# Local products on eight tiles from divided probabilities, and the output projection per four batches, in a recurrent attention scan

## The chip, the cores and the metric

The kernel runs on one core of a Trainium2 chip. The metric is the device time of one execution in microseconds (us). TensorE (PE in the profile) multiplies, VectorE (DVE), ScalarE (ACT) and POOL (GpSimd) work elementwise, SyncE (SP) issues the transfers. Every engine works through its own program in order; semaphores tie them together.

## What is computed

The program computes two blocks on 16 sequences of 512 tokens of 128 features. The change touches the second block alone, `scan`. Cut to that:

```python
# xn: layernorm of x; q, k, v = split(xn @ w_qkv), 16 heads of 64
for each segment of 32 tokens, in order:
    scores = q_rope @ k_rope.T * SCALE, causal mask
    sdpa   = softmax(scores) @ v
    sq, sk = elu(q) + 1, elu(k) + 1
    out    = beta * (sq @ mem) / (sq @ z + 1e-6) + (1 - beta) * sdpa
    mem   += sk.T @ (v - (sk @ mem) / (sk @ z))
    z     += sk.sum(tokens)
x = x + concat(out) @ w_out + fp8(xn) @ fp8(weight).T + bias
```

## The kernel before

The first block and the routing take the first half of the span. `scan` walks 16 segments x 8 pairs of heads, 128 pairs `p` in all. Every instruction works on all 16 sequences at once: four sequences (`f`) lie in the four groups of 32 partitions, and four groups `g` of these along the free axis, so that 128 partitions x 512 elements hold one pair.

The work is pipelined by hand. Each engine runs a loop over steps `s`, 128 plus 5 to drain; in step `s` it does the projection of pair `s`, the scores of pair `s - 1`, the recalls and local products of pair `s - 2`, the turning of the finished heads of `s - 3`, and the output projection and memory update of `s - 4`. The order inside a step is what the code writes; an engine that waits holds up all that follows. In one step:

- TensorE: `project` of the queries (L2016), `local` (L2050: probabilities times `uu`, which holds the values, 32 matmuls of 32 x 32 weights and 64 columns), `values` (L2022), `recall` of the keys (L2032), `turn_keys` (L2068), the mask (L2056) and `score` (L2061), `project` of the keys (L2016), `recall` of the queries (L2032), `project_out` (L2080), `turn_heads` (L2073), `update` (L2040). Once per segment it turns x and its fp8 copy (L1862, L1868), multiplies for the FFN (L2155) and turns the finished output (`turn_y`, L2085). A float32 matmul is two instructions of TensorE, so `local` is 64.
- ScalarE: `features` of the queries (L2165, L2170), the copy of the turned keys (L2179) and of the values into `uu` (L2183), the exponential of the scores (L2187), `features` of the keys (L2165, L2167, L2170), the copy of the turned heads into `oT` (L2199).
- VectorE: two instructions that take the local products out of PSUM and multiply them by 1 - beta and by the reciprocal of the softmax's sum (L2247), `rope` of the queries (L2219, L2220), `sigma_q` (L2226), the key recall divided (L2257, L2259), maximum and subtraction of the scores (L2264, L2265), the query recall divided into `t2` (L2276 to L2279), `rope` of the keys, then the 32 x 32 transposes of the exponentials into `pT` (L2285), their sum (L2287) and its reciprocal (L2288), and the memory's update (L2236).
- POOL: `rotate` of the queries (L1980, L1983), `sigma_k` (L1975), the subtraction of the recalled keys from `uu` (L1995), `rotate` of the keys, and `t2` added to the local products in `ol` (L2008).

PSUM banks 0 and 1 go round among q, v, k, x, the FFN and y; 2 and 3 hold the recalls, 4 and 5 the scores, 6 the local products and both kinds of transposes, 7 the output projection, which accumulates over the eight pairs of a segment.

## Time and profile before

| | us |
|---|---|
| median of 3 runs | 3138.38 (3136.64 to 3142.13) |
| span of the profiled execution | 3131.4 |
| TensorE busy | 2658.5 (85%) |
| VectorE busy | 2510.0 (80%) |
| ScalarE busy | 1876.0 (60%) |
| POOL busy | 1754.7 (56%) |

The device time of the profiled execution is not given beside its span; the runs' median is 7.0 us above the span. The span runs from the first to the last instruction. Busy time says how long instructions lay on an engine; TensorE's matmuls overlap, and their ends are modelled. In a timeline, the difference between two starts on one engine is what a piece costs there. "Idle before" is the time in which the engine had nothing, and the arrow names what ended it.

### The profile page before, as it was taken

How to read it: one execution, taken by the hardware profiler on the slowest of the kernel's cores; microseconds unless marked ns; L12 is line 12 of the kernel's file. 1: busy time of each engine (PE TensorE's matmuls, PEld its weight loads, DVE VectorE, ACT ScalarE, POOL GpSimd, SP SyncE). 2: the span in 40 equal slices, each digit the busy share in tenths (PEclk: the TensorE clock that was granted, in tenths of full speed). 3: DMA queues.
4: the chain of work that ended last, by engine and by line, in shares of the span. 5: the costliest groups of instructions: out<-in, count | busy, mean ns of one | idle time of the engine just before them, and what ended most of it. 6: DMA issues, size and time to landing. Idle time of an engine off the chain costs nothing. (4 is left out here: it accounts for less than half of the span.)

```text
span 3131.4 us, 129400 instructions
## 1 busy us (share of the span) xinstructions
PE 2658.5 (85%) x53553; PEld 1508.1 (48%) x53553; DVE 2510.0 (80%) x7597; ACT 1876.0 (60%) x3797; POOL 1754.7 (56%) x1984
## 2 busy tenths in 40 slices
PE   5884999999999999973340899999999999999998
PEld 2441333333333333363230566666666666666665
DVE  4676899999998999766706788888888888888886
ACT  5783899999999999821000455455555555555553
POOL 5871222222222222341063788888888888888886
PEclk9895999999999999986565999999999999999999
DMA  4676344333333343094023000000000000000000
GB/s 135 235 261 178 73 106 94 93 93 99 93 90 96 94 106 94 27 276 122 0 43 89 10 12 11 8 8 11 11 11 11 11 11 11 11 11 5 11 8 11
DMA packets 179263, 209.94 MB, mean 67 GB/s; under 512 B 28592, under 2 KB 140144, under 8 KB 178416
## 3 DMA queue, kind: packets, MB, share of 16 engines
q1 hardware_dynamic: 176112, 200.25, 23.1%
q8 instruction: 427, 7.00, 1.0%
q0 software_dynamic: 2560, 1.35, 0.4%
q14 instruction: 164, 1.34, 0.1%
HBM read 125.10 MB, written 75.63 MB: 64 GB/s over the span
## 5 line engine op out<-in xcount | busy, mean ns | idle before, releaser
L829 ACT ACTIVATE at_pA<-at_ps 128x512 f32<-128x512 f32 x1024 | 551.9, 614 | 83.8 <-DVE at_ps L882 77.1
L891 DVE CUSTOM_DVE_ANT_0 at_junk<-at_ps,w_cmask 128x512 f32<-128x512 f32 (+3 forms) x1024 | 463.4, 485 | 104.4 <-PE at_ps L732 97.1
L882 DVE TENSOR_TENSOR at_ps<-at_ps,w_ratio 128x128 f32<-128x128 f32 (+3 forms) x1024 | 451.2, 491 | 4.7 <-PE at_ps L726 3.1
L701 POOL TENSOR_SCALAR_AFFINE_SELECT at_pB<-at_pB 128x128 f32<-128x128 f32 x256 | 75.4, 294 | 639.6 <-ACT at_pB L835 637.5
L835 ACT ACTIVATE at_pB<-at_ps 128x512 f32<-128x512 f32 (+1 forms) x768 | 379.4, 531 | 53.0 <-PE at_ps L739 47.7
L1980 POOL TENSOR_TENSOR sc_rb<-sc_rb,v_sin 128x512 f32<-128x512 f32 x256 | 326.6, 1276 | 37.6 <-DVE sc_ra L2220 36.2
L2016 PE MATMUL sc_ps<-sc_xT,v_wqkv 128*128 128x512 f32 x512 | 286.1, 641 | 3.9 <-PEq L56 1.4
L726 PE MATMUL at_ps<-at_aq,at_ak 72*128 72x512 bf16 x1024 | 278.3, 388 | 2.7 <-DMA at_ak<-parts_scratch 2.4
L2179 ACT COPY sc_skN<-sc_ps 128x512 f32<-128x512 f32 x128 | 75.1, 587 | 323.6 <-PE sc_ps L2068 323.6
L1975 POOL TENSOR_TENSOR sc_sk<-sc_ee,sc_relu 128x512 f32<-128x512 f32 x128 | 167.0, 1304 | 180.5 <-ACT sc_ee L2170 180.3
L739 PE MATMUL at_ps<-at_bq,at_bk 75*128 75x512 bf16 (+3 forms) x1024 | 265.7, 302 | 1.5 <-ACT at_pB L835 0.9
L759 PE MATMUL at_ps<-at_pA,at_v 128*32 128x512 f32 x2048 | 263.0, 609 | 1.2 <-ACT at_oT L818 1.2
L732 PE MATMUL at_ps<-at_bk,at_bq 72*128 72x512 bf16 (+3 forms) x1024 | 225.1, 306 | 43.8 <-DMA at_bk<-parts_scratch 35.2
L2165 ACT ACTIVATE sc_ee<-sc_ps 128x512 f32<-128x512 f32 x256 | 150.4, 587 | 110.2 <-PE sc_ps L2016 109.0
L2219 DVE STREAM_SHUFFLE sc_rb<-sc_ps 128x512 f32<-128x512 f32 x256 | 189.1, 739 | 0.0
L2050 PEld LDWEIGHTS sc_ps<-v_uu,sc_pT 32*32 32x32 f32 x8192 | 125.4, 105 | 116.2 <-issue 109.1
L2220 DVE TENSOR_TENSOR sc_ra<-sc_ps,v_cos 128x512 f32<-128x512 f32 x256 | 172.3, 673 | 0.0
L1983 POOL TENSOR_TENSOR sc_kr<-sc_ra,sc_rb 128x512 f32<-128x512 f32 x128 | 163.1, 1274 | 10.0
L1983 POOL TENSOR_TENSOR sc_qr<-sc_ra,sc_rb 128x512 f32<-128x512 f32 x128 | 162.7, 1271 | 10.0
L2236 DVE TENSOR_TENSOR v_mem<-v_mem,sc_ps 128x520 f32<-128x520 f32 x256 | 161.8, 674 | 6.6 <-PE sc_ps L2040 6.6
L2008 POOL TENSOR_TENSOR sc_ol<-sc_ol,sc_t 128x512 f32<-128x512 f32 x128 | 163.2, 1275 | 5.9 <-DVE sc_t L2279 5.9
L2170 ACT ACTIVATE sc_ee<-sc_ee 128x512 f32<-128x512 f32 x256 | 161.4, 631 | 8.2
(316 smaller groups left out, 5937.4 us busy)
## 6 DMA issues: line engine op xcount, KB each, us to landing
parts_scratch<-fr_parts SPq DMA_DIRECT2D x64, 384.0 KB, 4.1
at_bq<-parts_scratch SPq DMA_DIRECT2D x192, 96.0 KB
at_bk<-parts_scratch SPq DMA_DIRECT2D x192, 96.0 KB
at_aq<-parts_scratch SPq DMA_DIRECT2D x192, 96.0 KB
at_ak<-parts_scratch SPq DMA_DIRECT2D x192, 96.0 KB
v_scratch<-fr_v SPq DMA_DIRECT2D x32, 352.0 KB, 4.3
at_v<-v_scratch SPq DMA_DIRECT2D x32, 352.0 KB, 3.6
parts_scratch<-fr_parts SPq DMA_DIRECT2D x32, 256.0 KB, 3.9
```

The lines of the kernel that those rows point to most:

```text
L726: pe.matmul(ps[:, BANK[f"A{j}"], :], ak[:, slot, n % 4, j * P:(j + 1) * P], aq[:, slot, n % 4], start=True, stop=True).then_inc(filled, 1)
L732: ins = pe.matmul(ps[:, BANK[kind], col:col + wide], bq[0:ROWS, slot, n % 4, j * P:(j + 1) * P], bk[0:ROWS, slot, n % 4, 0:wide], start=Tr ...
L739: ins = pe.matmul(ps[:, BANK[kind], col:col + S - j * P], bk[:, slot, n % 4, j * P:(j + 1) * P], bq[:, slot, n % 4, j * P:S], start=True, ...
L759: ins = pe.matmul(ps[32 * s:32 * s + 32, PV, q0:S], v[:, b % 2, a, j, h * (HD + 1):h * (HD + 1) + 32], probs, start=(j == 0), stop=(j == N ...
L829: act.activation(pA[:, n % A_RING, j * S:(j + 1) * S], src, ACT.Exp).then_inc(exped, 1)
L835: act.activation(pB[:, n % T_RING, at:at + wide], src[:, 0:wide], ACT.Exp).then_inc(exped, 1)
L882: dve.tensor_tensor(src[:, 0:wide], src[:, 0:wide], W["ratio"][:, S - wide:S], ALU.mult).then_inc(tilted, 1)
L891: ins = dve.tensor_tensor_reduce(junk[:, P * j * (j + 1) // 2:P * (j + 1) * (j + 2) // 2], src[:, col:col + wide], W["cmask"][:, S - wide: ...
L1980: pool.tensor_tensor(by_pos(rb[:, n % 2]), by_pos(rb[:, n % 2]), table("sin", which), ALU.mult).then_inc(G["sn"], 1)
L1983: pool.tensor_tensor(rot[which][:, p % 2], ra[:, n % 2], rb[:, n % 2], ALU.add).then_inc(G["add_d"], 1)
L2016: pe.matmul(ps[:, bank_of("qk"[which], p), :], V["wqkv"][:, col:col + P], xT[:, p // PAIRS % 2], start=True, stop=True).then_inc(G["pj"], 1)
L2219: dve.stream_shuffle(rb[:, n % 2], x, [lane ^ 1 for lane in range(32)])
```

## The change

1. `local` writes two banks instead of one. For the even groups `g` the products of the partitions of `f` go to the output partitions of `f`, in bank 6, as before; for the odd groups they go to those of `f ^ 1`, in bank 7. So there are eight pairs of rows and columns of the array in use instead of four. The query recall, the FFN's input (`take_xq`, three copies instead of one), the residual `hb` and the stored `y` follow that order of the partitions.
2. The probabilities are divided before they are multiplied. VectorE takes the sum and reciprocal before `rope` of the keys, POOL multiplies (a new instruction of 128 x 256), and VectorE transposes after `rope`.
3. ScalarE, no longer VectorE, takes the local products out of PSUM, scaled by 1 - beta; VectorE, no longer POOL, adds `t2`.
4. The output projection holds the tokens as weights. `oT` keeps all eight pairs of two segments. In each step from the 11th on, one half of one group `g` (four pairs) of a segment that is complete is multiplied: 4 matmuls of 128 columns into a quarter of bank 7. VectorE adds each half to `y` (128 x 128), and `local` and `project_out` of the next step wait for that (`ydone`). `turn_y`, the copy `yT` and the addition of 128 x 512 go.
5. The residual is loaded by transfers of its own into `hb` (`load_hb`), and stores are eight transfers per segment instead of four. The drain takes 10 steps instead of 5.

```diff
-        oT, yT = sb("oT", [P, 2, S]), sb("yT", [P, S])
+        oT = sb("oT", [P, 2, PAIRS, S])
...
+        by_ch = lambda ap: ap.rearrange("p (h g) -> p g h", h=2)
+        swapped = lambda g, f: f ^ (g % 2)
+        YCOL = 256
...
+        def load_hb(sp, seg, j):
+            for f in range(B1):
+                for odd in range(2):
+                    to = 32 * swapped(odd, f)
+                    sp.dma_start(hb[to:to + 32, j % 2, odd::2], h_seg[f, bass.ds(seg, 1)].rearrange("o i g d -> (o i) g d")[:, odd::2]).then_inc(G[f"hb_in{j % 2}"], 16)
...
-            wait_h(pool, j)
-            pool.tensor_tensor(hb[:, j % 2], ht[:, j % 2], V["bias"][:].unsqueeze(1).broadcast_to([P, BG, D]), ALU.add).then_inc(G["hb_d"], 1)
+            wait(pool, f"hb_in{j % 2}", 128 * max(1, (j + 1) // 2))
+            pool.tensor_tensor(hb[:, j % 2], hb[:, j % 2], V["bias"][:].unsqueeze(1).broadcast_to([P, BG, D]), ALU.add).then_inc(G["hb_d"], 1)
...
-            act.copy(xqT[:, j % 2], ps[:, bank, 0:256].bitcast(BF16)).then_inc(G["xqt_c"], 1)
+            place = lambda ap: ap.rearrange("p (q o a b i) -> p q o a b i", q=2, o=2, a=2, b=2)
+            to, at = place(xqT[:, j % 2]), place(ps[:, bank, 0:256].bitcast(BF16))
+            act.copy(to[:, :, 0].rearrange("p q a b i -> p q (a b i)"), at[:, :, 0].rearrange("p q a b i -> p q (a b i)"))
+            for b in range(2):
+                ins = act.copy(to[:, :, 1, :, 1 - b], at[:, :, 1, :, b])
+            ins.then_inc(G["xqt_c"], 1)
...
-        STEPS = PT + 5
+        HALVES, AFTER = 2 * BG, PAIRS + 2
+        STEPS = PT + AFTER
...
+        out_half = lambda s: (divmod((s - AFTER) % HALVES, 2), (s - AFTER) // HALVES) if inside(s - AFTER) else None
...
                     for j in range(PER):
-                        wait(sp, "ydone", j + 1)
-                        for f in range(B1):
-                            sp.dma_start(o_seg[f, bass.ds(seg + j, 1)].rearrange("o i g d -> (o i) g d"), y[32 * f:32 * f + 32, j % 2]).then_inc(G[f"stored{j % 2}"], 16)
                         if j + 3 in readied:
                             wait(sp, "xnn_d", j + 1)
-                            wait(sp, "hb_d", j + 1)
                             load(sp, seg + j + 3, j + 3)
+                        if j + 2 in readied:
+                            wait(sp, "ffn_c", j + 1)
+                            load_hb(sp, seg + j + 2, j + 2)
+                        wait(sp, "ydone", HALVES * (j + 1))
+                        for f in range(B1):
+                            for odd in range(2):
+                                at = 32 * swapped(odd, f)
+                                sp.dma_start(o_seg[f, bass.ds(seg + j, 1)].rearrange("o i g d -> (o i) g d")[:, odd::2], y[at:at + 32, j % 2, odd::2]).then_inc(G[f"stored{j % 2}"], 16)
...
+                            wait(pool, "smd", p + 1)
+                            probs = ss[:, p % 2].rearrange("p (g h) j -> p g h j", h=2)
+                            pool.tensor_tensor(probs, probs, bc(by_ch(sm[:, p % 4]), SEG), ALU.mult).then_inc(G["nrm"], 1)
...
-                            wait(pool, "ffn_c", j - 1)
                             add_bias(pool, j)
-                        p = s - 2
-                        if inside(p):
-                            wait(pool, "qd", p + 1)
-                            wait(pool, "old", p + 1)
-                            o = ol[:, p % 4].rearrange("p g h d -> p (g h d)")
-                            pool.tensor_tensor(o, o, t2[:, p % 2].rearrange("p c d -> p (c d)"), ALU.add).then_inc(G["od"], 1)
 
...
-                                    ins = pe.matmul(ps[32 * f:32 * f + 32, 2 + hh, g * VE:(g + 1) * VE],
+                                    to = 32 * (swapped(g, f) if which == 0 else f)
+                                    ins = pe.matmul(ps[to:to + 32, 2 + hh, g * VE:(g + 1) * VE],
...
                     def local(p):
-                        for g in range(BG):
-                            for hh in range(2):
+                        for hh in range(2):
+                            for g in range(BG):
                                 for f in range(B1):
-                                    ch = 2 * g + hh
-                                    ins = pe.matmul(ps[32 * f:32 * f + 32, 6, ch * DH:(ch + 1) * DH], pT[32 * f:32 * f + 32, p % 4, ch, :],
+                                    ch, to, col = 2 * g + hh, 32 * swapped(g, f), (2 * (g // 2) + hh) * DH
+                                    ins = pe.matmul(ps[to:to + 32, 6 + g % 2, col:col + DH], pT[32 * f:32 * f + 32, p % 4, ch, :],
                                                     uu[32 * f:32 * f + 32, p % PAIRS, g, hh, 0:DH], start=True, stop=True)
...
-                    def project_out(p):
-                        wait(pe, "otc", p + 1)
-                        wait(pe, "yt_c", p // PAIRS)
-                        h = p % PAIRS
-                        pe.matmul(ps[:, 7, :], V["wout"][:, h], oT[:, p % 2], start=(h == 0), stop=(h == PAIRS - 1)).then_inc(G["oproj"], 1)
-
-                    def turn_y(bank, j):
-                        wait(pe, "yt_c", j + 1)
-                        for g in range(BG):
-                            ins = pe.transpose(ps[:, bank, g * P:(g + 1) * P], yT[:, g * P:(g + 1) * P], V["ident"][:])
-                        ins.then_inc(G["yt"], 1)
+                    def project_out(j, g, half):
+                        few = range(half * PAIRS // 2, (half + 1) * PAIRS // 2)
+                        for h in few:
+                            ins = pe.matmul(ps[:, 7, YCOL:YCOL + D], oT[:, j % 2, h, g * P:(g + 1) * P], V["wout"][:, h], start=(h == few[0]), stop=(h == few[-1]))
+                        ins.then_inc(G["oproj"], 1)
...
+                            wait(pe, "ydone", s - AFTER)
                             wait(pe, "pt", p + 1)
                             local(p)
...
-                        p = s - 4
-                        if inside(p):
-                            project_out(p)
+                        if out_half(s):
+                            (g, half), j = out_half(s)
+                            wait(pe, "old", min(s - 1, PT))
+                            wait(pe, "otc", j * PAIRS + 4 * half + 4)
+                            wait(pe, "ydone", s - AFTER)
+                            project_out(j, g, half)
...
+                            wait(act, "pvd", p + 1)
+                            wait(act, "ott", p - 3)
+                            local = ps[:, 6:8, 0:256].rearrange("p b (q h d) -> p b q h d", h=2, d=DH)
+                            to = ol[:, p % 4].rearrange("p (q b) h d -> p b q h d", b=2)
+                            for hh in range(2):
+                                col = 2 * (p % PAIRS) + hh
+                                ins = act.activation(to[:, :, :, hh], local[:, :, :, hh], ACT.Identity, scale=V["rest"][:, col:col + 1])
+                            ins.then_inc(G["old"], 1)
...
-                            wait(dve, "pvd", p + 1)
-                            wait(dve, "pt", p + 1)
-                            wait(dve, "ott", p - 3)
-                            local = ps[:, 6, :].rearrange("p (g h d) -> p g h d", h=2, d=DH)
-                            for hh in range(2):
-                                col = 2 * (p % PAIRS) + hh
-                                ins = dve.scalar_tensor_tensor(ol[:, p % 4, :, hh], local[:, :, hh], V["rest"][:, col:col + 1],
-                                                               bc(head(sm[:, p % 4])[:, hh], DH), ALU.mult, ALU.mult)
-                            ins.then_inc(G["old"], 1)
...
+                        p = s - 3
+                        if inside(p):
+                            wait(dve, "old", p + 1)
+                            wait(dve, "qd", p + 1)
+                            o = ol[:, p % 4].rearrange("p g h d -> p (g h d)")
+                            dve.tensor_tensor(o, o, t2[:, p % 2].rearrange("p c d -> p (c d)"), ALU.add).then_inc(G["od"], 1)
...
+                        p = s - 1
+                        if inside(p):
+                            wait(dve, "se", p + 1)
+                            s_ = sm[:, p % 4]
+                            link(dve.tensor_reduce(head(s_), by_head(ss[:, p % 2]), AX.X, ALU.add))
+                            dve.reciprocal(s_, s_).then_inc(G["smd"], 1)
                         if s < PT:
                             rope(2 * s + 1)
                         p = s - 1
                         if inside(p):
-                            wait(dve, "se", p + 1)
-                            dve.transpose(pT[:, p % 4].rearrange("p c j -> p (c j)"), ss[:, p % 2].rearrange("p c j -> p (c j)"))
-                            s_ = sm[:, p % 4]
-                            link(dve.tensor_reduce(head(s_), by_head(ss[:, p % 2]), AX.X, ALU.add))
-                            dve.reciprocal(s_, s_).then_inc(G["pt"], 1)
+                            wait(dve, "nrm", p + 1)
+                            dve.transpose(pT[:, p % 4].rearrange("p c j -> p (c j)"), ss[:, p % 2].rearrange("p c j -> p (c j)")).then_inc(G["pt"], 1)
                         if s - 7 in starts:
                             j = (s - 7) // PAIRS
                             wait(dve, "ffn", j + 1)
                             wait(dve, "hb_d", j)
-                            wait(dve, f"stored{j % 2}", 64 * (j // 2))
+                            wait(dve, f"stored{j % 2}", 128 * (j // 2))
                             dve.scalar_tensor_tensor(flat(y[:, j % 2]), ps[:, bank_of("ffn", j), :], V["qs"][:, 4:5], flat(hb[:, j % 2]),
                                                      ALU.mult, ALU.add).then_inc(G["ffn_c"], 1)
-                        if s - 12 in starts:
-                            j = (s - 12) // PAIRS
-                            wait(dve, "yt", j + 1)
+                        if out_half(s):
+                            (g, half), j = out_half(s)
+                            wait(dve, "oproj", s - AFTER + 1)
                             wait(dve, "ffn_c", j + 1)
-                            dve.tensor_tensor(flat(y[:, j % 2]), flat(y[:, j % 2]), ps[:, bank_of("y", j), :], ALU.add).then_inc(G["ydone"], 1)
+                            wait(dve, "ydone", s - AFTER)
+                            dve.tensor_tensor(y[:, j % 2, g], y[:, j % 2, g], ps[:, 7, YCOL:YCOL + D], ALU.add).then_inc(G["ydone"], 1)
```

The order on POOL in the steady state, from the rotation of the queries to that of the next step's. `sc_sk` is what `sigma_k` writes, `v_uu` the subtraction's, `sc_ss` the probabilities, `sc_ol` the local products. Before:

```order
L1980 TENSOR_TENSOR sc_rb<-sc_rb,v_sin 128x512
L1983 TENSOR_TENSOR sc_qr<-sc_ra,sc_rb 128x512
L1975 TENSOR_TENSOR sc_sk<-sc_ee,sc_relu 128x512
L1995 TENSOR_TENSOR v_uu<-v_uu,sc_t 128x8x64
L1980 TENSOR_TENSOR sc_rb<-sc_rb,v_sin 128x512
L1983 TENSOR_TENSOR sc_kr<-sc_ra,sc_rb 128x512
L2008 TENSOR_TENSOR sc_ol<-sc_ol,sc_t 128x512
```

With the change:

```order
L2001 TENSOR_TENSOR sc_rb<-sc_rb,v_sin 128x512
L2004 TENSOR_TENSOR sc_qr<-sc_ra,sc_rb 128x512
L1996 TENSOR_TENSOR sc_sk<-sc_ee,sc_relu 128x512
L2016 TENSOR_TENSOR v_uu<-v_uu,sc_t 128x8x64
L2021 TENSOR_TENSOR sc_ss<-sc_ss,sc_sm 128x256
L2001 TENSOR_TENSOR sc_rb<-sc_rb,v_sin 128x512
L2004 TENSOR_TENSOR sc_kr<-sc_ra,sc_rb 128x512
```

The addition into `sc_ol` is gone from the end, and the multiply of the probabilities stands behind the subtraction from `v_uu`.

The order on VectorE from the maximum of the scores to the memory's update (`sc_mx` maximum, `sc_rq` reciprocal of the query recall, `sc_sm` sums, `sc_pT` the transposed probabilities). Before:

```order
L2264 TENSOR_REDUCE sc_mx<-sc_ps 128x8
L2265 TENSOR_TENSOR sc_ss<-sc_ps,sc_mx 128x2x4x32
L2276 SCALAR_TENSOR_TENSOR sc_rq<-sc_ps,v_ibeta 128x8
L2277 RECIPROCAL sc_rq<-sc_rq 128x8
L2279 TENSOR_TENSOR sc_t<-sc_ps,sc_rq 128x2x4x64
L2219 STREAM_SHUFFLE sc_rb<-sc_ps 128x512
L2220 TENSOR_TENSOR sc_ra<-sc_ps,v_cos 128x512
L2285 STREAM_TRANSPOSE sc_pT<-sc_ss 128x256
L2287 TENSOR_REDUCE sc_sm<-sc_ss 128x8
L2288 RECIPROCAL sc_sm<-sc_sm 128x8
L2236 TENSOR_TENSOR v_mem<-v_mem,sc_ps 128x2x4x65 x2
```

With the change:

```order
L2273 TENSOR_REDUCE sc_mx<-sc_ps 128x8
L2274 TENSOR_TENSOR sc_ss<-sc_ps,sc_mx 128x2x4x32
L2286 TENSOR_TENSOR sc_ol<-sc_ol,sc_t 128x512
L2291 SCALAR_TENSOR_TENSOR sc_rq<-sc_ps,v_ibeta 128x8
L2292 RECIPROCAL sc_rq<-sc_rq 128x8
L2294 TENSOR_TENSOR sc_t<-sc_ps,sc_rq 128x2x4x64
L2299 TENSOR_REDUCE sc_sm<-sc_ss 128x8
L2300 RECIPROCAL sc_sm<-sc_sm 128x8
L2239 STREAM_SHUFFLE sc_rb<-sc_ps 128x512
L2240 TENSOR_TENSOR sc_ra<-sc_ps,v_cos 128x512
L2306 STREAM_TRANSPOSE sc_pT<-sc_ss 128x256
L2319 TENSOR_TENSOR sc_y<-sc_y,sc_ps 128x128
```

Sum and reciprocal stand before the rotation, the transpose behind it, and the addition of a finished half to `sc_y` follows the transpose.

## Rows read from the trace of the kernel before

**Rows 1.** The page, busy us (share of span) and slices of the span: TensorE

```profile
PE 2658.5 (85%) x53553; PEld 1508.1 (48%) x53553; DVE 2510.0 (80%) x7597; ACT 1876.0 (60%) x3797; POOL 1754.7 (56%) x1984
...
PEclk9895999999999999986565999999999999999999
```

**Rows 2.** The view of line L2050 (`local`), all of it

```profile
L2050 PE MATMUL sc_ps<-v_uu,sc_pT x8192: 211/214/312, 1739.9 to 3114.3; 32*32 32x64 f32 x200
```

**Rows 3.** Timeline of one step, TensorE: start us, us busy, engine, line, instructions [idle before]

```profile
2043.46 1.10 PE L2050 MATMUL sc_ps<-v_uu,sc_pT 32*32 32x64 f32 x64
...
2044.50 1.16 PE L2022 MATMUL sc_ps<-v_wqkv,sc_xT 128*128 128x128 f32 x8
...
2045.58 0.86 PE L2032 MATMUL sc_ps<-v_mem,sc_sk 64*32 64x65 f32 x64
...
2046.38 0.66 PE L2068 MATMUL sc_ps<-v_ident,sc_sk 128*128 128x128 f32 x4
...
2047.07 0.71 PE L2061 MATMUL sc_ps<-sc_kr,sc_qr 64*32 64x32 f32 x59
...
2048.58 0.25 PE L2061 MATMUL sc_ps<-sc_kr,sc_qr 64*32 64x32 f32 x5 [0.80 <-issue]
2048.76 1.12 PE L2016 MATMUL sc_ps<-sc_xT,v_wqkv 128*128 128x512 f32 x2
...
2050.61 1.13 PE L2080 MATMUL sc_ps<-sc_oT,v_wout 128*128 128x512 f32 x2
...
2054.19 0.60 PE L2050 MATMUL sc_ps<-v_uu,sc_pT 32*32 32x64 f32 x28
```

**Rows 4.** Timeline of the same step, the other engines

```profile
2051.16 0.69 DVE L2279 TENSOR_TENSOR sc_t<-sc_ps,sc_rq 128x512 f32<-128x512 f32 x1
2051.22 0.63 ACT L2170 ACTIVATE sc_ee<-sc_ee 128x512 f32<-128x512 f32 x1
...
2051.93 1.28 POOL L1975 TENSOR_TENSOR sc_sk<-sc_ee,sc_relu 128x512 f32<-128x512 f32 x1 [2.49 <-ACT sc_ee L2170]
...
2053.00 0.43 DVE L2285 STREAM_TRANSPOSE sc_pT<-sc_ss 128x256 f32<-128x256 f32 x1
2053.16 1.19 POOL L1995 TENSOR_TENSOR v_uu<-v_uu,sc_t 128x512 f32<-128x512 f32 x1
...
2053.36 0.37 DVE L2287 TENSOR_REDUCE sc_sm<-sc_ss 128x8 f32<-128x256 f32 x1
```

**Rows 5.** Timeline of another step: T and `sigma_k`

```profile
2416.86 1.12 PE L2016 MATMUL sc_ps<-sc_xT,v_wqkv 128*128 128x512 f32 x2
...
2420.38 1.28 POOL L1975 TENSOR_TENSOR sc_sk<-sc_ee,sc_relu 128x512 f32<-128x512 f32 x1 [1.70 <-ACT sc_ee L2170]
```

**Rows 6.** Groups by form: line engine op out<-in xcount | busy, mean ns | idle before

```profile
L1980 POOL TENSOR_TENSOR sc_rb<-sc_rb,v_sin 128x512 f32<-128x512 f32 x256 | 326.6, 1276 | 37.6 <-DVE sc_ra L2220 36.2
...
L704 POOL TENSOR_SCALAR_AFFINE_SELECT at_pB<-at_pB 128x384 f32<-128x384 f32 x256 | 133.8, 523 | 0.1
...
L241 POOL TENSOR_TENSOR fr_sc<-fr_sc 128x8 f32<-128x8 f32 x8 | 1.6, 203 | 0.0
...
L864 DVE TENSOR_TENSOR at_on<-at_ps,at_rr 128x128 f32<-128x128 f32 x128 | 37.4, 292 | 4.4
...
L835 ACT ACTIVATE at_pB<-at_ps 128x256 f32<-128x256 f32 x256 | 98.1, 383 | 0.0
```

**Rows 7.** Groups by form of the window 1735 to 3115 us, TensorE

```profile
L2050 PE MATMUL sc_ps<-v_uu,sc_pT 32*32 32x64 f32 x8192 | 147.0, 216 | 15.9 <-DVE sc_sm L2288 9.7 <-issue 3.5
...
L2032 PE MATMUL sc_ps<-v_mem,sc_sk 64*32 64x65 f32 x8184 | 116.0, 225 | 14.0 <-issue 13.8
...
L2061 PE MATMUL sc_ps<-sc_kr,sc_qr 64*32 64x32 f32 x8154 | 103.3, 199 | 15.7 <-issue 15.0
```

**Rows 8.** Timeline of the end, ScalarE and VectorE

```profile
3122.36 0.59 ACT L2199 COPY sc_oT<-sc_ps 128x512 f32<-128x512 f32 x1 [1.75 <-PE sc_ps L2073]
...
3127.08 0.68 DVE L2300 TENSOR_TENSOR sc_y<-sc_y,sc_ps 128x512 f32<-128x512 f32 x1
```

28 lines of the change are left out of this document (11 added, 17 removed).

## The prediction, as made before the run

> **What bounds the kernel now.** I began with the page's busy shares and its slices [rows 1]. TensorE is busiest with 85% of the span, and from the 23rd slice (22 x 78.3 = 1722 us) to the last its clock stands at nine tenths or more of full speed, so at the 2.4 GHz level nearly throughout. The change touches only `scan`, which begins there, so I looked at nothing else. Next the rows of the line of `local`, which runs once per step (a step is one pair of heads of one segment; there are 128): the 128 bursts begin between 1739.9 and 3114.3 us, and the last burst begins at about 3113.4, so one step takes (3113.4 - 1739.9) / 127 = **10.82 us** [rows 2].
>
> Then I took one ordinary step apart. On TensorE [rows 3] it runs from the first `local` at 2043.46 to the next at 2054.19, which is 10.73 us. Start to start: `local` 1.04, values 1.08, recall of the keys 0.80, `turn_keys` and mask 0.69, `score`, and only then the projection of the keys, whose start I call T (2048.76). `score` took 1.69, of which 1.00 was a stop in its middle with no wait in the program (the profile says "issue"): its first 59 instructions take 0.51 without the last one's own 0.20, the other five 0.18, so 0.69 packed. Local to T is thus 4.30 packed and 5.30 here. From T: key projection and recall of the queries 1.85, output projection 0.96, then `turn_heads`, update, the transposes of one ready segment and the next query projection, up to T + 5.43, where the next `local` starts. So TensorE is nearly packed; I read it as the bound, with VectorE (80% of the whole span) close behind.
>
> On the other engines [rows 4] the same step has a chain which starts at T. ScalarE gets the projected keys and does two Relus and an Exp, the Exp starting at T + 2.46; POOL can then start `sigma_k` at T + 3.17 and, right behind it, the subtraction from `uu`, which ends at T + 5.59 (2053.16 + 1.19). Before the change nobody who holds up `local` waits for that: `local` needs the transposed probabilities, which VectorE begins at T + 4.24. This is where the change bites.
>
> **The change, part by part.**
>
> *Division of the probabilities on POOL.* The sum and the reciprocal move ahead of the rotation on VectorE, then POOL multiplies, then VectorE transposes. POOL runs strictly in program order, and the new multiply stands behind `sigma_k` and the subtraction from `uu`. So its inputs may be ready at about T + 3.7 (t2 ends at T + 3.1 [rows 4], then a sum and a reciprocal), but it starts at the end of the subtraction: T + 5.59 in this step. In another step `sigma_k` started at T + 3.52 instead of T + 3.17 [rows 4, 5], which with the same 2.42 for the two makes T + 5.94; VectorE was late there with work that the change takes off it, so I take 5.67. Nothing in the trace shows the multiply. Its nearest rows on POOL are 523 ns for a select over 384 elements per lane and 1276 ns for a multiply of 512 with a broadcast operand; an 8-element multiply takes 203 ns [rows 6]. The line between 203 and 1276 gives 203 + 1073 x 248/504 = 731 ns for its 256 elements. I take **0.73**, between 0.52 and 1.28.
>
> *What then stands before `local`.* A handoff to VectorE (0.08, as from the Exp's end at 2051.85 to `sigma_k` at 2051.93 [rows 4]), the transpose (0.36 start to start [rows 4]), and, new, the addition of the finished half of the output, since `local` also waits for `ydone` of the step before: 292 ns for 128 x 128 [rows 6], and 0.10 for the handoff to TensorE. Sum 0.73 + 0.08 + 0.36 + 0.29 + 0.10 = 1.56. In one step of eight the FFN's instruction on 512 elements stands between the transpose and that addition; at the 0.68 of a like-sized addition [rows 8] that is 0.09 on average. `local` then starts at T + 5.67 + 1.56 + 0.09 = **T + 7.32**, where the packed TensorE would be there at T + 5.4. Nothing covers that wait: all of TensorE is queued behind it, values, recalls and the next T included, and ScalarE, POOL and VectorE wait for these. The wait closes a loop: T, ScalarE, POOL, VectorE, `local`, next T.
>
> *Eight tiles instead of four in `local`.* Before, 64 instructions start every 16 ns on four tiles (1.04 us). The recalls, also 64 instructions, of 65 columns on eight tiles and two banks, take 0.80; `score` with 32 columns takes 0.69 [rows 3]. I take 0.80: **-0.24** inside the loop. Bounds: -0.35 and 0. The profile shows four tiles in different row groups writing one bank with starts 16 ns apart and 214 ns each [rows 2, 3], so they do overlap. The Trainium skill (TensorEngine Tiling (Array Packing), Restrictions and Gotchas) says that different row tiles cannot access the same bank at the same time. The new form still has four row groups in each of two banks. By that rule `local` would not get shorter. It is the third rival.
>
> *The loop's length.* Local to T: 4.30 - 0.24 = 4.06, plus pauses. TensorE idles 14.0 us before the key recall and 15.7 us before `score` in 128 steps, 0.23 per step; the listing sees 0.80 of the 1.00 lost in the example [rows 3, 7], so 0.30. The step becomes 4.06 + 0.30 + 7.32 = **11.68 us**, 0.86 more than 10.82. Over 125 steps: **+107 us**. The pauses in the other half (recall of the queries) vanish in the wait and are not in this sum.
>
> *Output projection, tokens held.* Four matmuls of 128 columns (two instructions each, like the values' 1.08) for one of 512 (0.96 [rows 3]): +0.12 per step, between T and `local`, where there are now 1.9 us of slack: nothing. The four transposes of `turn_y` and the copy of `yT` per segment go, also there: nothing. Hidden by the wait for the probabilities; without it the sum would be -0.24 + 0.12 - 0.06 = -0.18 per step.
>
> *Evacuation of the local products.* From two VectorE instructions (0.80 us) to two ScalarE ones. A 128 x 256 activation from PSUM takes 383 ns [rows 6]. They start when `local` ends and `turn_keys` needs them 1.9 us after that (values and key recall); 0.8 us fits. The addition into `ol` moves from POOL to VectorE, in the gap in which VectorE waits for the query recall. POOL and VectorE both get less work than before. Nothing.
>
> *More DMAs.* The residual is loaded a second time (8 transfers per segment), the stores are 8 instead of 4. They are issued some steps ahead; DMA is nearly idle in `scan`. Nothing, but for half a microsecond behind the last store.
>
> *The end.* The last 8 halves of the projection come out one per step with nothing beside them: after the last copy into `oT` seven remain, each 1.08 of matmuls, 0.2 until the result is there, 0.29 addition, 0.1 handoff, 1.65 x 7 = 11.6. Before, from that copy's end (3122.36 + 0.59) to the end of the last addition (3127.08 + 0.68) it took 4.8 [rows 8]. With the longer chain in the two draining steps and half a microsecond of stores I take **+10**.
>
> Sum: 107 + 10 = +117. The span shown is 3131.4; the median of the runs is 3138.4, 7 us more, which I keep. Forecast 3138.4 + 117 = **3255 us**.
>
> **The rivals.**
> 1. *The multiply is covered and TensorE stays the bound.* Then only TensorE's sum counts: -0.18 x 128 = -23, and +10 at the end: 3125, faster. The point from which it decides: POOL's path must deliver `local` no later than TensorE itself gets there, mean 10.82 - 4.60 = T + 6.2 with the pauses; it needs 1.1 us less than my 7.32. For it: the wait ends only 1.1 us after the mean. Against: POOL's subtraction alone ends at T + 5.6 in an undisturbed step, before multiply, transpose and addition. 9%.
> 2. *The pauses before T disappear*, since TensorE's queue fills while it waits: 0.30 x 125 = 38 less: 3217. For it: they come in dense stretches. 20%.
> 3. *Eight tiles are no faster than four*: 0.24 x 128 = +31: 3286. 10%.
> 4. *The multiply costs as much as one of 512*: +0.55 x 125 = +69: 3324. 8%.
> 5. *It balances out*, rival 1 with half its gain lost to new waits in one step of eight (the rounding of a segment delays VectorE, and the addition into `ol` with it): about 3138. 3%.
>
> **How the numbers follow.** My forecast has 50%, with the rivals 9, 20, 10, 8 and 3. Cheapest plausible combination of bounds: multiply 0.52 (-26), no pauses (-38): 3191, so the range begins at 3190; it ends at 3325 with rival 4. A measurement of this kernel can tell about 0.2%, some 6 us, from no change. Faster 0.09, same 0.03, slower 0.88.
>
> **What would show it.** TensorE's idle time in front of `local` should rise from 15.9 us [rows 7] to over 150, released by VectorE (its transpose or the half's addition), and POOL's new multiply should start within 0.1 us of the end of the subtraction. `local` should take 0.8 us; the idle time before the query recall should stay or shrink. POOL and VectorE shares of `scan` fall while the step grows to 11.7 us. I am wrong if the step is under 10.8 us, or if the multiply is not found right behind the subtraction, or if `local` is found waiting for ScalarE.

## The result, and the profile after

The changed kernel takes **3269.7 us** (median of 4 runs, 3265.8 to 3282.8) where the kernel before takes 3140.3 in the same comparison (4 runs, 3136.6 to 3144.0): a ratio of 1.0416, 95% interval 1.0394 to 1.0439. Its profiled execution has a span of 3263.6 us against 3131.4. One run of the kernel before, among those beside e5 to e8, took 3725.1 us at a mean granted clock of 0.64 (0.93 in the others) and is left out of all ratios. The page's busy shares and granted clock:

```profile
PE 2660.1 (82%) x54257; PEld 1561.6 (48%) x54257; DVE 2513.9 (77%) x7581; ACT 1973.7 (60%) x4069; POOL 1674.9 (51%) x1984
...
PEclk9995999999999999865658999999999999999999
```

TensorE lies as long in its instructions as before (2660.1 us against 2658.5) in a span that is 132 us longer, and its granted clock in the loop is nearly the same (0.99 from 1800 to 3100 us, 1.00 before): the time is waiting. The line of `local`, with what ended TensorE's idle time before it (us, times):

```profile
L2070 PE MATMUL sc_ps<-v_uu,sc_pT x8192: 210/215/312, 1743.3 to 3234.7; 32*32 32x64 f32 x200
...
  DVE sc_y L2319: 112.2, 100
  DVE sc_pT L2306: 22.7, 9
```

Before, the idle time there was 15.9 us in all [rows 7]. The groups of the whole scan stretch (busy us and mean ns, then idle us before them and who ended it), of TensorE and then of the new chain:

```profile
L2052 PE MATMUL sc_ps<-v_mem,sc_sq 64*32 64x65 f32 x8192 | 120.6, 225 | 24.7 <-issue 23.1 <-DVE sc_t L2268 1.0
...
L2052 PE MATMUL sc_ps<-v_mem,sc_sk 64*32 64x65 f32 x8192 | 118.0, 228 | 23.6 <-issue 23.6
L2070 PE MATMUL sc_ps<-v_uu,sc_pT 32*32 32x64 f32 x8192 | 115.1, 226 | 127.9 <-DVE sc_y L2319 112.2 <-DVE sc_pT L2306 13.7 <-issue 1.9
...
L2021 POOL TENSOR_TENSOR sc_ss<-sc_ss,sc_sm 128x256 f32<-128x256 f32 x128 | 80.5, 629 | 3.6 <-DVE sc_sm L2300 3.6
...
L2306 DVE STREAM_TRANSPOSE sc_pT<-sc_ss 128x256 f32<-128x256 f32 x128 | 57.0, 445 | 105.5 <-POOL sc_ss L2021 104.5
```

Idle before `local` is 127.9 us, ended by VectorE's addition of the half (L2319) or its transpose (L2306). The transpose itself waits 105.5 us, for POOL's multiply; the multiply waits 3.6, so POOL's program holds it, not its inputs. An ordinary step, from one `local` to the next (start, duration):

```profile
2131.74 0.85 PE L2070 MATMUL sc_ps<-v_uu,sc_pT 32*32 32x64 f32 x64 [0.34 <-DVE sc_y L2319]
...
2133.60 0.69 PE L2052 MATMUL sc_ps<-v_mem,sc_sk 64*32 64x65 f32 x45
...
2135.01 0.41 PE L2052 MATMUL sc_ps<-v_mem,sc_sk 64*32 64x65 f32 x19 [0.71 <-issue]
...
2136.74 1.12 PE L2035 MATMUL sc_ps<-sc_xT,v_wqkv 128*128 128x512 f32 x2
...
2137.80 0.57 PE L2052 MATMUL sc_ps<-v_mem,sc_sq 64*32 64x65 f32 x35
...
2139.06 0.45 PE L2052 MATMUL sc_ps<-v_mem,sc_sq 64*32 64x65 f32 x29 [0.69 <-issue]
...
2139.90 1.28 POOL L1996 TENSOR_TENSOR sc_sk<-sc_ee,sc_relu 128x512 f32<-128x512 f32 x1 [3.12 <-ACT sc_ee L2184]
...
2141.14 1.19 POOL L2016 TENSOR_TENSOR v_uu<-v_uu,sc_t 128x512 f32<-128x512 f32 x1
...
2142.28 0.63 POOL L2021 TENSOR_TENSOR sc_ss<-sc_ss,sc_sm 128x256 f32<-128x256 f32 x1
...
2142.94 0.45 DVE L2306 STREAM_TRANSPOSE sc_pT<-sc_ss 128x256 f32<-128x256 f32 x1 [0.40 <-POOL sc_ss L2021]
...
2143.31 0.25 DVE L2319 TENSOR_TENSOR sc_y<-sc_y,sc_ps 128x128 f32<-128x128 f32 x1
...
2143.66 0.38 PE L2070 MATMUL sc_ps<-v_uu,sc_pT 32*32 32x64 f32 x19 [0.72 <-DVE sc_y L2319]
```

T is 2136.74. `sigma_k` (L1996) starts at T + 3.16, the subtraction (L2016) ends at T + 5.59, and the multiply stands in POOL's queue right behind it, at T + 5.54 (the records of POOL overlap by 0.05). It takes 0.63; transpose, addition and handoffs take 0.75 more, and `local` starts at T + 6.92, after a wait of 0.72. In this step both recalls (L2052) have a stop without a wait, of 0.7 us.

The end of the span, with the halves of the output projection one after the other, and TensorE's granted clock in it (the column before the DMA share):

```profile
3242.70 1.97 PE L2099 MATMUL sc_ps<-v_wout,sc_oT 128*128 128x128 f32 x8
...
3245.53 0.59 ACT L2219 COPY sc_oT<-sc_ps 128x512 f32<-128x512 f32 x1 [3.36 <-PE sc_ps L2093]
...
3255.32 1.13 PE L2099 MATMUL sc_ps<-v_wout,sc_oT 128*128 128x128 f32 x8 [0.47 <-DVE sc_y L2319]
...
3256.92 1.13 PE L2099 MATMUL sc_ps<-v_wout,sc_oT 128*128 128x128 f32 x8 [0.47 <-DVE sc_y L2319]
3258.09 0.29 DVE L2319 TENSOR_TENSOR sc_y<-sc_y,sc_ps 128x128 f32<-128x128 f32 x1 [1.31 <-PE sc_ps L2099]
```

```profile
3240.00:3245.00 5.00, 4.81 (x82) 4.20 (x80) 2.47 (x5) 0.58 (x1) 0.00 (x0) 0.56 0.19 46
3245.00:3263.60 18.60, 10.06 (x188) 8.60 (x187) 4.43 (x11) 0.59 (x1) 0.00 (x0) 0.94 0.07 17
```

**Where the 132 us of span lie.** The first `local` starts 3.4 us later (1739.9, then 1743.3). The first instruction of the last `local` moves from 3113.4 to 3232.0, so that 127 steps take 1488.7 us instead of 1373.5: 11.72 each instead of 10.82, **115.2 us**. From there to the end it is 31.6 us instead of 18.0: **13.6**. The first term is hardly the change's: over all kernels below, the first `local` starts between 1737.5 and 1750.0, and for the nine that have this change's transfers and output projection between 1737.5 and 1745.8. What moves it is not isolated; the clock in the 23 us before it is low in both kernels, 0.80 here (the third column from the end) and 0.82 before:

```profile
1722.00:1745.00 23.00, 12.57 (x167) 7.84 (x168) 12.27 (x35) 10.09 (x21) 12.86 (x11) 0.80 0.13 36
```

### The profile page after: what moved, and what is told of

Read it like the earlier page. It is cut to its first block and busy times, and to the rows that moved or that the text cites. A ratio compares the mean times of both kernels' runs of the same rounds, so it can differ in the third digit from the quotient of the medians.

```text
span 3263.6 us, 131202 instructions
## 1 busy us (share of the span) xinstructions
PE 2660.1 (82%) x54257; PEld 1561.6 (48%) x54257; DVE 2513.9 (77%) x7581; ACT 1973.7 (60%) x4069; POOL 1674.9 (51%) x1984
## 3 DMA queue, kind: packets, MB, share of 16 engines
q14 instruction: 169, 1.38, 0.2%
## 5 line engine op out<-in xcount | busy, mean ns | idle before, releaser
L1996 POOL TENSOR_TENSOR sc_sk<-sc_ee,sc_relu 128x512 f32<-128x512 f32 x128 | 170.5, 1332 | 330.5 <-ACT sc_ee L2184 330.5
L2035 PE MATMUL sc_ps<-sc_xT,v_wqkv 128*128 128x512 f32 x512 | 291.8, 653 | 17.0 <-DVE sc_ra L2240 12.8
L2070 PE MATMUL sc_ps<-v_uu,sc_pT 32*32 32x64 f32 x8192 | 115.1, 226 | 127.9 <-DVE sc_y L2319 112.2
L2070 PEld LDWEIGHTS sc_ps<-v_uu,sc_pT 32*32 32x32 f32 x8192 | 94.3, 105 | 231.6 <-issue 220.8
L2240 DVE TENSOR_TENSOR sc_ra<-sc_ps,v_cos 128x512 f32<-128x512 f32 x256 | 172.6, 674 | 0.0
```

Of the source, the lines that this page charges most:

```text
L1996: pool.tensor_tensor(sig[1][:, p % 4], ee[:, 1], relu[:], ALU.add).then_inc(G["sgk"], 1)
L2035: pe.matmul(ps[:, bank_of("qk"[which], p), :], V["wqkv"][:, col:col + P], xT[:, p // PAIRS % 2], start=True, stop=True).then_inc(G["pj"], 1)
```

## The experiments

All ratios are to the kernel before, run beside them on the same chip. "Step" is the mean over 110 steps, from the starts of `local`; A is the part from `local` to T, B from T to the next `local`; "stops" is the time per step in pauses inside TensorE's bursts that no wait explains; then TensorE's busy time per step, and its idle time per step that the profile says VectorE ended, before whatever instruction. These are worked out from all TensorE records of a trace. The last three do not add up to the step exactly: ends of matmuls are modelled, and short gaps are left out.

| kernel | us | ratio, 95% interval | step | A | B | stops | TensorE busy | waits for VectorE | last `local` to end |
|---|---|---|---|---|---|---|---|---|---|
| before | | 1 | 10.83 | 4.77 | 6.05 | 0.71 | 10.04 | 0.18 | 18.0 |
| changed | 3269.7 | 1.0416 (1.0394 to 1.0439) | 11.71 | 4.59 | 7.12 | 0.66 | 9.95 | 1.19 | 31.6 |
| e1 | 3203.3 | 1.0216 (1.0189 to 1.0242) | 11.26 | 4.76 | 6.50 | 0.97 | 9.93 | 0.48 | 31.6 |
| e2 | 3243.5 | 1.0354 (1.0332 to 1.0376) | 11.58 | 4.63 | 6.95 | 0.83 | 9.90 | 0.97 | 31.4 |
| e3 | 3275.7 | 1.0452 (1.0430 to 1.0474) | 11.83 | 4.71 | 7.12 | 0.61 | 10.12 | 1.17 | 31.5 |
| e4 | 3187.3 | 1.0171 (1.0144 to 1.0199) | 11.15 | 4.73 | 6.42 | 0.93 | 9.94 | 0.38 | 31.4 |
| e5 | 3150.7 | 1.0084 (1.0068 to 1.0101) | 10.85 | 4.50 | 6.35 | 0.65 | 9.91 | 0.39 | 31.5 |
| e6 | 3151.3 | 1.0083 (1.0061 to 1.0105) | 10.89 | 4.59 | 6.30 | 0.50 | 10.07 | 0.41 | 31.4 |
| e7 | 3257.4 | 1.0423 (1.0397 to 1.0449) | 11.73 | 4.66 | 7.07 | 0.41 | 10.18 | 1.21 | 17.5 |
| e8 | 3363.9 | 1.0771 (1.0743 to 1.0800) | 12.53 | 4.85 | 7.67 | 0.36 | 10.37 | 1.84 | 31.2 |
| e9 | 3144.3 | 1.0034 (1.0019 to 1.0048) | 10.87 | 4.65 | 6.22 | 0.51 | 10.04 | 0.37 | 17.1 |
| e10 | 3131.8 | 1.0001 (0.9986 to 1.0016) | 10.76 | 4.51 | 6.25 | 0.36 | 10.06 | 0.39 | 18.4 |
| e11 | 3151.0 | 1.0050 (1.0029 to 1.0071) | 10.88 | 4.44 | 6.45 | 0.64 | 9.44 | 0.94 | 28.0 |

The kernel before takes 3132.7 beside e1 to e4 (7 runs), 3124.0 beside e5 to e8 (11), 3132.3 beside e9 to e11 (26). So times of different groups are compared by their ratios.

### e1: the multiply ahead of the subtraction from `uu`

```diff
                             sigma_k(s)
+                        p = s - 1
+                        if inside(p):
+                            wait(pool, "smd", p + 1)
...
+                            pool.tensor_tensor(probs, probs, bc(by_ch(sm[:, p % 4]), SEG), ALU.mult).then_inc(G["nrm"], 1)
                         p = s - 2
...
                             pool.tensor_tensor(new, new, t1[:, p % 2].rearrange("p (g h) d -> p g h d", h=2), ALU.subtract).then_inc(G["ud"], 1)
-                        p = s - 1
-                        if inside(p):
-                            wait(pool, "smd", p + 1)
...
```

> The changed kernel (3269.7 us) with one thing moved: POOL multiplies the probabilities behind sigma_k and before the subtraction from uu, not behind it. Theory (loop T, ScalarE, POOL, VectorE, local): the multiply starts at about T + 4.4 (or when the reciprocal is ready, T + 3.8 to 4.6) instead of T + 5.6, the addition of the half ends 0.7 us later or a bit more, and local is reached at about T + 6.2, mostly TensorE's own time. The step falls from 11.7 to about 10.7 us, 127 steps, so 3145 us, range 3115 to 3165. Rival (the cost lies in TensorE's own work, the output projection in 128-column pieces or the new tile order): within 10 us of 3270.

About half of the loss goes (1.0416 to 1.0216), not nearly all of it. A step of e1, the T of which is 2130.15:

```profile
2130.15 1.13 PE L2035 MATMUL sc_ps<-sc_xT,v_wqkv 128*128 128x512 f32 x2
...
2132.10 0.17 DVE L2291 SCALAR_TENSOR_TENSOR sc_rq<-sc_ps,v_ibeta 128x8 f32<-128x8 f32 x1 [0.36 <-PE sc_ps L2052]
...
2132.90 1.05 PE L2099 MATMUL sc_ps<-v_wout,sc_oT 128*128 128x128 f32 x8 [0.84 <-issue]
...
2134.35 0.68 DVE L2240 TENSOR_TENSOR sc_ra<-sc_ps,v_cos 128x512 f32<-128x512 f32 x1
...
2134.54 0.63 POOL L2015 TENSOR_TENSOR sc_ss<-sc_ss,sc_sm 128x256 f32<-128x256 f32 x1
...
2135.16 1.13 PE L2035 MATMUL sc_ps<-sc_xT,v_wqkv 128*128 128x512 f32 x2
2135.20 0.45 DVE L2306 STREAM_TRANSPOSE sc_pT<-sc_ss 128x256 f32<-128x256 f32 x1 [0.17 <-POOL sc_ss L2015]
2135.57 0.25 DVE L2319 TENSOR_TENSOR sc_y<-sc_y,sc_ps 128x128 f32<-128x128 f32 x1
...
2136.22 0.98 PE L2070 MATMUL sc_ps<-v_uu,sc_pT 32*32 32x64 f32 x64
```

The multiply now starts at T + 4.39, but `local` only at T + 6.07. In this step it does not wait at all: it follows the projection of the queries (2135.16), and TensorE had stopped for 0.84 us ahead of `project_out`. Over the scan a wait is left, less than a third of the changed kernel's:

```profile
L2070 PE MATMUL sc_ps<-v_uu,sc_pT 32*32 32x64 f32 x8192 | 116.0, 223 | 39.9 <-DVE sc_y L2319 24.4 <-DVE sc_pT L2306 8.8 <-issue 6.2
```

VectorE works down a program of its own that starts when the query recall lands: its division, `t2`, the sum (L2299), the reciprocal, the rotation (L2240 ends it), and only then the transpose and the addition (L2306, L2319). In the step shown it ends 0.4 us before TensorE gets to `local`; in others it ends later. The mean of B falls by 0.62 only. By the table e1's step is 0.43 longer than the kernel before's for two reasons of like size: 0.30 more waits for VectorE, and 0.26 more stops, with 0.11 less busy time against them.

### e2: the half's addition ahead of the transpose

```diff
                             rope(2 * s + 1)
+                        if out_half(s):
...
+                            dve.tensor_tensor(y[:, j % 2, g], y[:, j % 2, g], ps[:, 7, YCOL:YCOL + D], ALU.add).then_inc(G["ydone"], 1)
                         p = s - 1
                         if inside(p):
                             wait(dve, "nrm", p + 1)
...
-                        if out_half(s):
...
```

> The changed kernel with VectorE's addition of the finished half moved ahead of its wait for the multiplied probabilities, so that the addition lies in that wait. Theory: the 0.25 us start to start (and the FFN's instruction's share, no longer between transpose and addition) leave the loop: 0.3 us in some 118 steps, -35 us, so 3235 us; local is then released by the transpose. Rival (local waits for the products of something else, or the end of the addition is not what it waits for): 3270.

The addition's input (from L2099) has long been there, so it fits in front of the wait for POOL: 0.6% come back, 20 us of the 35 expected. B falls by 0.17, and the stops grow by as much (0.66 to 0.83), partly in A. `local` now waits for the transpose alone:

```profile
L2070 PE MATMUL sc_ps<-v_uu,sc_pT 32*32 32x64 f32 x8192 | 113.6, 223 | 105.7 <-DVE sc_pT L2312 103.8 <-issue 1.6
```

### e3: four tiles in `local` again

```diff
-        swapped = lambda g, f: f ^ (g % 2)
+        swapped = lambda g, f: f
...
-                ins = act.copy(to[:, :, 1, :, 1 - b], at[:, :, 1, :, b])
+                ins = act.copy(to[:, :, 1, :, b], at[:, :, 1, :, b])
```

> The changed kernel with local on the four diagonal tiles again, still alternating between the two banks, all partitions in their old order. Theory: local takes 1.04 instead of 0.80 us, inside the loop, so +0.24 x 127 = +30 us, 3300 us. Rival (TensorE is not on the loop in this part, or two banks and not eight tiles shorten local): 3270.

The burst takes 1.03 us instead of 0.78 (medians to the next instruction), inside the loop, where the wait stays as long:

```profile
L2070 PE MATMUL sc_ps<-v_uu,sc_pT 32*32 32x64 f32 x8192 | 147.4, 218 | 125.6 <-DVE sc_y L2319 110.5 <-DVE sc_pT L2306 13.7 <-issue 1.3
```

Since e3 keeps the two banks, it is the eight tiles and not the second bank that shorten the burst. Of the 0.25 only 0.12 reach the step: 0.4% of the time by the runs (its interval just overlaps the changed kernel's), 15 us by the traces, instead of the 31 that 0.24 x 128 gives. In e5 against e6 they bring nothing.

### e4: the division left out

```diff
-                            pool.tensor_tensor(probs, probs, bc(by_ch(sm[:, p % 4]), SEG), ALU.mult).then_inc(G["nrm"], 1)
...
-                            wait(dve, "nrm", p + 1)
+                            wait(dve, "smd", p + 1)
```

Its output lacks the division of the softmax; the sum and reciprocal are still worked out.

> The changed kernel without POOL's multiply: the probabilities stay undivided (that part of the computation is left out), VectorE transposes when its rotation is done. Theory: local is reached at about T + 5.8 to 6.2, where TensorE's own work with its pauses ends; step 10.5 to 10.6 us, so about 3130 us, and nearly the same as with the early multiply. Rival (TensorE's own work carries the loss): above 3240.

Even without the multiply 1.7% stay, where the theory expected nothing. Of the 1.7%, 0.4 are the drain. The wait before `local` is 28.1 us, against 15.9 in the kernel before:

```profile
L2065 PE MATMUL sc_ps<-v_uu,sc_pT 32*32 32x64 f32 x8192 | 115.7, 223 | 28.1 <-DVE sc_y L2314 14.4 <-DVE sc_pT L2301 7.7 <-issue 4.9
```

By the table the step is 0.32 longer than before: 0.20 more waits for VectorE (before `local`, `turn_heads` and a projection) and 0.22 more stops, with 0.10 less busy time. That VectorE's new *order* costs without the new instruction is therefore not shown: e5, with another order, waits for VectorE as long (0.39), and what it has less than e4 is stops (0.65 against 0.93).

### e5 and e6: all of it off the chain

VectorE takes sum and reciprocal while it waits for the query recall; POOL multiplies while it waits for ScalarE's exponential, ahead of `sigma_k`; VectorE transposes and adds the half ahead of the rotation. e6 is the same with e3's four tiles.

```diff
                             rotate(2 * s)
+                        p = s - 1
+                        if inside(p):
+                            wait(pool, "smd", p + 1)
...
+                            pool.tensor_tensor(probs, probs, bc(by_ch(sm[:, p % 4]), SEG), ALU.mult).then_inc(G["nrm"], 1)
                         if s < PT:
                             sigma_k(s)
...
+                            link(dve.tensor_reduce(head(s_), by_head(ss[:, p % 2]), AX.X, ALU.add))
+                            dve.reciprocal(s_, s_).then_inc(G["smd"], 1)
                         p = s - 2
                         if inside(p):
                             wait(dve, "qr_s", p + 1)
...
+                            wait(dve, "nrm", p + 1)
...
+                            dve.tensor_tensor(y[:, j % 2, g], y[:, j % 2, g], ps[:, 7, YCOL:YCOL + D], ALU.add).then_inc(G["ydone"], 1)
                         if s < PT:
                             rope(2 * s + 1)
```

> The changed kernel with VectorE's sum and reciprocal moved into its wait for the query recall, POOL's multiply ahead of sigma_k (POOL is idle there), and VectorE's transpose and the half's addition ahead of its rotation of the keys. No instruction is added or left out. Theory: local can start from about T + 4 on, so that the loop is gone and TensorE's own work is the bound: 9.55 us packed plus the stops inside bursts, which were 0.7 per step before and 0.97 in e1, so a step of 10.5 and about 3120 us, range 3095 to 3150; idle before local under 20 us in all. Rival (the loss sits in the new output projection and its additions): still above 3180.

> As e5, with local on four tiles. Theory: with TensorE as the bound the 0.24 us of local count in every step, less what the stops give back: e3 cost 0.12 per step with the loop, of which 0.24 is local and -0.1 are fewer stops. Between +10 and +30 us over e5. Rival (eight tiles bring nothing, since a denser burst only meets a later block of instructions): within 5 us of e5.

With the same instructions in this order 3.3% come back, and 0.8% stay. In e5's scan the wait before `local` is gone, and the transpose no longer waits for POOL:

```profile
L2060 PE MATMUL sc_ps<-v_uu,sc_skN 32*64 32x65 f32 x8192 | 122.0, 234 | 30.9 <-DVE sc_t L2300 26.2 <-issue 3.7 <-DVE v_mem L2256 0.5
...
L2070 PE MATMUL sc_ps<-v_uu,sc_pT 32*32 32x64 f32 x8192 | 114.7, 224 | 9.2 <-issue 5.2 <-DVE sc_pT L2304 3.3
...
L2093 PE MATMUL sc_ps<-v_ident,sc_ol 128*128 128x128 f32 x512 | 79.1, 277 | 17.2 <-DVE sc_ol L2286 15.4 <-issue 1.8
...
L2304 DVE STREAM_TRANSPOSE sc_pT<-sc_ss 128x256 f32<-128x256 f32 x128 | 55.7, 435 | 2.5 <-POOL sc_ss L2013 2.5
```

The loop is back at 10.85 against 10.83. The span differs from before by 21.4: 2.8 in the loop, 5.1 before the first `local`, 13.5 after the last. The theory expected 3120. Its idle time before `local` came out, but TensorE still waits 0.39 us per step for VectorE in other places (before the update and `turn_heads` above all), which the theory left out. The multiply isn't quite free for POOL either: on average it ends at T + 3.47, and `sigma_k` starts at T + 3.61 instead of T + 3.18, but the loop does not show it (10.85).

e6 is equal to e5: its rival came true. TensorE is busy 0.16 us longer per step and stops 0.15 less.

### e7: the kernel before, with the division alone

Sum and reciprocal before the rotation, POOL's multiply behind the subtraction, the transpose after the rotation; tiles, projection and evacuation of the kernel before (its evacuation without the reciprocal).

```diff
+                            wait(pool, "smd", p + 1)
+                            probs = ss[:, p % 2].rearrange("p (g h) j -> p g h j", h=2)
+                            pool.tensor_tensor(probs, probs, bc(sm[:, p % 4].rearrange("p (h g) -> p g h", h=2), SEG), ALU.mult).then_inc(G["nrm"], 1)
...
-                                ins = dve.scalar_tensor_tensor(ol[:, p % 4, :, hh], local[:, :, hh], V["rest"][:, col:col + 1],
-                                                               bc(head(sm[:, p % 4])[:, hh], DH), ALU.mult, ALU.mult)
+                                ins = dve.tensor_scalar(ol[:, p % 4, :, hh], local[:, :, hh], V["rest"][:, col:col + 1], None, ALU.mult)
```

> The kernel before with one part of the change alone: sum and reciprocal before VectorE's rotation, POOL's multiply behind the subtraction from uu, the transpose after the rotation, the local products then scaled by 1 - beta alone. Output projection, tiles and the engines of evacuation stay as they were. Theory: local at T + 5.6 + 0.63 + 0.05 + 0.45 + 0.1 = T + 6.8, the step 4.7 + 6.8 = 11.5 to 11.6 us, so +90 us on the kernel before: 3225, range 3200 to 3250. Rival (the loss needs the new output projection): within 20 us of the kernel before.

This one part gives the **whole** loss, 1.0423, with the same step (11.73) and the same wait:

```profile
L2055 PE MATMUL sc_ps<-v_uu,sc_pT 32*32 32x64 f32 x8192 | 151.6, 222 | 127.0 <-DVE sc_pT L2295 126.5
...
L2000 POOL TENSOR_TENSOR sc_ss<-sc_ss,sc_sm 128x256 f32<-128x256 f32 x128 | 80.5, 629 | 4.0 <-DVE sc_sm L2289 4.0
```

It is more than the 90 us expected: the multiply starts at T + 5.72 on average where the theory had 5.6, and `local` at T + 7.07 where it had 6.8. In the loop the rest takes as much as it gives: the eight tiles give 0.12 per step (e3), the half's addition in the chain takes 0.13 (e2). Only the drain is left, 17.5 us here against 31.6: the span of e7 is 3253.1, 10.5 less than the changed kernel's, which the ratios, from different groups, don't resolve.

### e8: the multiply twice

```diff
+                            pool.tensor_tensor(waste[:].rearrange("p (g h) j -> p g h j", h=2), probs, bc(by_ch(sm[:, p % 4]), SEG), ALU.mult)
                             pool.tensor_tensor(probs, probs, bc(by_ch(sm[:, p % 4]), SEG), ALU.mult).then_inc(G["nrm"], 1)
```

> The changed kernel with POOL's multiply done twice (once into a buffer that nobody reads). Theory: POOL's multiply lies on the loop at full price, +0.59 us start to start in 127 steps, +75 us on the changed kernel: 3340. Rival (the multiply is partly covered): clearly less, under +45.

The step grows by 0.82, more than the 0.59 between the starts of the two multiplies. The group of `local` in e8, and its window of the scan:

```profile
L2072 PE MATMUL sc_ps<-v_uu,sc_pT 32*32 32x64 f32 x8192 | 118.0, 232 | 209.1 <-DVE sc_y L2321 187.4 <-DVE sc_pT L2308 20.5 <-issue 1.2
```

```profile
1800.00:3330.00 1530.00, 1262.55 (x42909) 932.16 (x42908) 1136.96 (x2783) 769.59 (x1525) 1097.47 (x1004) 0.94 0.04 11
```

The wait before `local` grows by 81 us, 0.64 per step, which is the multiply; it lies in B, which grows by 0.55. A grows by 0.26. The rest is TensorE itself: its granted clock over the scan is 0.94, where the changed kernel has 0.99. It idles longer in each step, and in part of the steps it is then at the 1.2 GHz level: values and projections last longer (1.38 instead of 1.12 us per step for the values).

### e9: the kernel before, with only sum and reciprocal early

```diff
+                            wait(dve, "se", p + 1)
+                            s_ = sm[:, p % 4]
+                            link(dve.tensor_reduce(head(s_), by_head(ss[:, p % 2]), AX.X, ALU.add))
+                            link(dve.reciprocal(s_, s_))
                         p = s - 2
                         if inside(p):
                             wait(dve, "qr_s", p + 1)
...
-                            link(dve.tensor_reduce(head(s_), by_head(ss[:, p % 2]), AX.X, ALU.add))
-                            dve.reciprocal(s_, s_).then_inc(G["pt"], 1)
```

> The kernel before, with one thing moved: VectorE adds the two halves of the sums of exponentials and takes their reciprocals before it waits for the recalled query, as in e5. The transposition follows, then the rope's addition; nothing else changes. Theory (in the kernel before, VectorE's chain that starts when the query's recall lands is late at the local product by 15.9 us over the loop, 0.12 us per step, and the two small operations on it are worth about 0.2): the idle time before the local product falls below 8 us and the kernel takes 3118 to 3132 us where the kernel before takes 3132, a ratio of 0.996 to 1.000. Rival (the same chain also feeds VectorE's next work, which TensorE waits for elsewhere): ratio under 0.994. Rival (the reciprocal now waits for ScalarE's exponential and holds the query's addition up): over 1.002.

```profile
L2050 PE MATMUL sc_ps<-v_uu,sc_pT 32*32 32x64 f32 x8192 | 145.4, 217 | 8.1 <-DVE sc_pT L2290 6.4 <-issue 1.6
...
L2040 PE MATMUL sc_ps<-v_uu,sc_skN 32*64 32x65 f32 x8192 | 119.8, 232 | 49.0 <-DVE sc_t L2285 45.6 <-issue 1.7 <-DVE v_mem L2236 0.5
```

The same line of the kernel before, in the same stretch:

```profile
L2040 PE MATMUL sc_ps<-v_uu,sc_skN 32*64 32x65 f32 x8192 | 120.6, 232 | 24.1 <-DVE sc_t L2279 19.5 <-issue 4.0 <-DVE v_mem L2236 0.5
```

The wait before `local` halves [rows 7], and the one before the memory's update (L2040), which needs the query recall done with (L2285), goes from 24.1 to 49.0: the sum and the reciprocal now stand ahead of that division. It is 0.3% slower, as the last rival had it, and the theory of a gain falls. Of that the loop accounts for 7 us (1380.3 against 1373.5); its first `local` also starts 10 us later in the trace. VectorE's chain feeds TensorE in two places, and moving work from one to the other is no gain.

### e10: the division off the chain, projection and tiles of before

e6 with `project_out`, `turn_y`, `yT`, residual and stores of the kernel before:

```diff
-                            project_out(j, g, half)
+                            project_out(p)
...
-                            act.copy(oT[:, p // PAIRS % 2, p % PAIRS], ps[:, 6, :]).then_inc(G["otc"], 1)
+                            act.copy(oT[:, p % 2], ps[:, 6, :]).then_inc(G["otc"], 1)
```

> e6 (four tiles; sum, reciprocal, multiply, transposition and addition off the chain, as in e5) with the output projection of the kernel before: no tokens held, one projection per two batches and its old evacuation. So it is the kernel before with the division made on the probabilities, off the chain. Theory (the last 0.8% of e5 and e6 over the kernel before are the held tokens' longer drain, 31.5 us against 18.0, and some 0.1 us per step of the projection per four batches): the drain is back at 18 to 20 us, the step is 10.75 to 10.85, and the time is 3125 to 3140 us where the kernel before takes 3132, ratio 0.998 to 1.002. Rival (the division itself costs outside the chain, by the VectorE and GpSimd work it adds to the step): the loop stays at 10.89 and only the drain comes back: ratio 1.003 to 1.006. Rival (the chain off the query's recall was the bound of the kernel before too): ratio under 0.996.

```profile
L2049 PE MATMUL sc_ps<-v_uu,sc_pT 32*32 32x64 f32 x8192 | 142.9, 216 | 4.2 <-DVE sc_pT L2292 3.3 <-issue 0.9
```

1.0001, interval 0.9986 to 1.0016: no difference from the kernel before. The drain is 18.4 us, and the step 10.76, 0.13 less than e6. So the 0.8% of e6 is the new output projection with its residual and stores: its drain (13 us) and 0.1 us per step. The latter isn't matmul work: TensorE is busy as long in both (10.06 and 10.07); the stops are 0.36 instead of 0.50. And the division, placed so and with ScalarE's evacuation, costs nothing on balance: against the kernel before TensorE waits 0.21 us more per step for VectorE and stops 0.35 less. Nothing tried beats the kernel before by more than the measurement can tell.

### e11: e5 with a quarter of the output projection

One of the four matmuls of each half is left; the output lacks the other three pairs' parts.

```diff
-                        for h in few:
-                            ins = pe.matmul(ps[:, 7, YCOL:YCOL + D], oT[:, j % 2, h, g * P:(g + 1) * P], V["wout"][:, h], start=(h == few[0]), stop=(h == few[-1]))
+                        for h in (few[0],):
+                            ins = pe.matmul(ps[:, 7, YCOL:YCOL + D], oT[:, j % 2, h, g * P:(g + 1) * P], V["wout"][:, h], start=True, stop=True)
```

> e5 with three of the four matmuls of each half of the output projection left out, so that its output lacks those parts of the sum. TensorE's output projection (2.33 us per step) falls to about 0.6. Theory (with the division off the chain TensorE's own work is the bound again, nothing else is near it): nearly all of it comes back, 1.6 us per step over 120 steps, and 2 us in the drain: 2950 to 2990 us where e5 has 3151. Rival (the step is held by the chain through softmax, query recall and transposition, just under TensorE's work): less than half of it comes back, the idle time before the local product is back above 60 us, and the time is over 3060. Rival (stops inside TensorE's bursts shrink with the instructions they depend on): under 2940.

The expectation's 2.33 us per step for the projection was wrong: it is 151.6 us in all in e5, 1.2 per step, and 65.5 here. But even these 86 us bring nothing in the loop: its step is 10.88, not less. Part of them TensorE does not gain at all: its granted clock from 1800 to 3100 us is 0.97 where e5 has 0.99, its other groups take longer (L2060: 241 ns instead of 234), and its busy time falls by 0.47 us per step, 60 us in the loop. The 0.3% to e5 are its drain (28.0 us) and a first `local` 4.3 us earlier.

```profile
L2060 PE MATMUL sc_ps<-v_uu,sc_skN 32*64 32x65 f32 x8192 | 126.0, 241 | 73.8 <-DVE sc_t L2300 68.4 <-issue 4.2 <-DVE v_mem L2256 1.0
...
L2093 PE MATMUL sc_ps<-v_ident,sc_ol 128*128 128x128 f32 x512 | 80.8, 282 | 36.3 <-DVE sc_ol L2286 35.9 <-issue 0.2
...
L2099 PE MATMUL sc_ps<-v_wout,sc_oT 128*128 128x128 f32 x256 | 65.5, 340 | 4.8 <-DVE sc_y L2310 2.8 <-issue 1.9
```

Idle time before the update (L2060) goes from 30.9 to 73.8 us and before `turn_heads` (L2093) from 17.2 to 36.3, both ended by VectorE. All of TensorE's waits for VectorE grow by 0.55 us per step, as much as its busy time falls. So the step of e5 does not hang on TensorE's own work alone: with less of it, the chain through the query recall and VectorE holds the step at the same 10.8 us, which the first of the two rivals named (though the wait shows before L2060 and L2093, and the one before `local` is 5.2 us, not over 60). Whether TensorE's work holds it too, no run shows: e6, which adds to that work, also stops less.

## Why the prediction was right, and where not

The forecast was 3255, the time is 3269.7, inside 3190 to 3325. By its own steps:

- **POOL's multiply behind the subtraction bites.** Right, in place and size: e7 shows that it alone gives the whole loss, e5 and e10 that with sum, multiply and transpose in other places of the programs the loop loses nothing. `sigma_k` starts at T + 3.16, the multiply at T + 5.53 (median; forecast 5.67).
- **The multiply at 0.73.** It takes 0.63 (0.59 start to start, e8). Rival 4 (the price of 512 elements) falls.
- **What then stands before `local`, 1.56.** It takes 1.38 in the medians: the multiply 0.66 with its handoff, the transpose 0.37, addition and handoff 0.35. Median start T + 6.91, mean T + 7.12 (forecast 7.32). The step of the forecast that failed is "there are now 1.9 us of slack": TensorE gets to `local` 1.0 us before the probabilities (127.9 us over the loop), where the packed sum had 1.9. The forecast left out of that half what TensorE still meets there, some 0.5 us per step: idle time before the query recall (24.7 us, nearly all stops; 30.3 in the kernel before), the projections (17.0), `turn_heads` (14.4) and the update (12.8). With the projection's 0.12 that is most of the difference. The threshold of "over 150" for that idle time was therefore wrong.
- **Stops before T, 0.30.** They are 0.40 in the bursts from `local` to `score`, and A is 4.59 instead of 4.36. This error (+0.23) and the one in B (-0.20) cancel: 4.59 + 7.12 = 11.71 against 11.68. That the step came out to 0.03 us is luck; each half is right to 0.2. Rival 2 (the stops disappear) falls: TensorE's waits didn't take them away.
- **Eight tiles, -0.24.** The burst shortens as forecast, 1.03 to 0.78. The Trainium skill (TensorEngine Tiling (Array Packing), Restrictions and Gotchas) says that different row tiles cannot access one bank at the same time; by that `local` could not be shorter in a form with all four row groups in each bank. The traces disagree: 1.03 and 0.78. Yet rival 3 was half right about the time: the step gains only 0.12 (e3), and in the loop of e5 and e6 nothing.
- **Projection, evacuation, transfers: nothing.** In the changed kernel's loop that holds (no wait before L2099 beyond 6.5 us). Behind the wait it isn't nothing: e6 against e10 shows 0.13 us per step, as much as their difference in stops, and the drain.
- **The end, +10.** It is 13.6. From the copy's end (3246.12) to the last addition's end (3258.38) 12.3 us against 4.8, where the forecast had 11.6: the halves follow each other in 1.60, not 1.65. The rest is in the steps before, 4.6 us longer. 1.8 of them are a stop inside the last `local` (from 3232.8 to 3234.6), though the kernel before has one of 0.9 in its last query recall; another part is the clock, 0.56 from 3240 to 3245 where the kernel before has 1.00 from 3113 to 3123: the half at 3242.70 takes 1.97 instead of 1.16. The stores take 1.6 more.
- **Rival 1, which had the other sign**, needed B at 6.2. e1 and e4 show that it was further away than the sum said: with the multiply further ahead, or without it, B is still 6.4 to 6.5. In both TensorE waits for VectorE's program in several places (0.38 to 0.48 us per step) and stops more. I had not priced that. e5's B is 6.35 and its loop only equals the old one.
- **The sum, +117.** The spans differ by 132.2: 8 more in the loop (115.2 against 107), 3.6 at the end, and 3.4 before the first `local`, for which I had no term.

My theories of e1, e4 and e5 all expected too much, for one reason: I took POOL's chain for one bound and TensorE's own packed work for the next. Between them lies VectorE's chain from the query recall, which feeds TensorE before the update, `turn_heads` and `local`, and e11 shows that taking work from TensorE alone moves nothing against it. And the stops change with every variant, from 0.36 to 0.97 us per step, by as much as most of the effects looked for; a difference of 0.1 to 0.3 us per step between two variants can be stops alone.

Two things stay open: a version in which TensorE's stops are gone, and what TensorE's own work would allow if VectorE's chain were shorter.

## What to carry to other kernels

When an operation is put on an engine that works in program order, its price is decided by its place: the same division (a sum, a reciprocal, a multiply of 0.63 us and a transpose) costs 4% with the multiply behind the subtraction that waits for this step's exponential, and nothing with the multiply ahead of `sigma_k`, where POOL mostly waits anyway, and VectorE's parts moved to fit. Before crediting a gain to the removal of one wait, follow every engine's program to the same consumer: here POOL's chain, VectorE's and TensorE's own work ended within about one microsecond, and the first experiments uncovered the next one instead of the gain. A pipeline that holds results for a later batch pays at its end, here 13 us.

## What the runs showed of the hardware

**TensorE stops inside bursts, at a fixed time after a transfer of instructions.** The pauses that the profile gives to "issue" have a common time. In the steps read from a trace, every kernel shows them ending 2.5 us (5% to 95%: 2.2 to 2.8) after the start of a 16 KB transfer on the queue of kind "instruction", and 1.4 us (1.2 to 1.55) after it landed; this holds for 93 stops of the changed kernel, 95 of the one before, 121 of e1 and 52 of e10. Moments taken at random in the same steps of the changed kernel lie anywhere from 0.2 to 4.4 us after such a start. Such a transfer starts every 4.2 us on average there, with 276 weight loads and matmuls between two (median). For the stop that ends at 2139.06 in the step above, the transfers between 2136 and 2138 in 40 slices of 0.05 us:

```profile
GB/s 0 0 0 0 0 0 328 0 0 0 0 0 0 0 0 0 0 0 0 0 0 0 0 0 0 0 0 0 0 0 0 0 0 0 0 0 0 0 0 0
...
q8 instruction: 1, 0.02, 4.5%
```

The one packet starts in the seventh slice, at 2136.3, 2.7 us before the stop's end. That the transfers cause the stops is argued from this timing; no run changes them. It would explain why denser bursts give back part of what they gain: e1 and e4, whose steps are shorter with the same TensorE instructions, have 0.93 to 0.97 us of stops per step where the changed kernel has 0.66, and going from four tiles to eight the stops rise from 0.61 to 0.66 (e3) and from 0.50 to 0.65 (e6, e5). They are not a simple function of the step's length (e7 has 0.41, e10 0.36).

**More waiting can cost clock.** e8's granted clock in the scan is 0.94 against 0.99 in the changed kernel, with waits for VectorE of 1.84 us per step against 1.19, and the step grew by 0.2 us more than the wait. e11's is 0.97 against 0.99 in e5, with 0.94 against 0.39. The wait alone does not settle it: the changed kernel waits longer than e11 and has 0.99.
